# Second FFN of a hybrid block: GpSimd gathers the rows of four experts, not six, before its first scatter

## What is computed

```
xn   = rmsnorm(x) * norm_weight              # 4096 tokens x 128
probs = softmax(xn @ router_weight.T + router_bias)   # 16 experts
_, idx = top_k(logits.T, 256)                # each expert picks 256 tokens
xe = xn[idx]                                 # 16 x 256 x 128
h  = gelu(xe @ fc1.T + fc1_bias)             # 512 wide
y  = h @ fc2.T + fc2_bias
output = zeros.at[idx].add(y * gates)        # scatter-add over the experts
output = output / sum of the gates           # where a token was picked
```

## Time and profile before

| | before |
|---|---|
| median of 3 runs | 690.29 us |
| the profiled execution's own time | 692.55 us |
| its span | 690.8 us |
| mean granted TensorE clock | 0.766 |
| busy: VectorE, TensorE, GpSimd, ScalarE | 61%, 55%, 52%, 32% |
| the second FFN's experts, first gather to last scatter | 566.6 to 684.9 us |
| the first FFN's experts, first gather to last scatter | 224.7 to 329.5 us |

### The profile page before, as it was taken

How to read it: one execution, slowest core, us unless ns; L and a number is a source line. 1 busy time by engine, 2 the same in 40 slices (tenths; PEclk the granted TensorE clock), 3 DMA queues, 4 the chain that set the end, 5 groups by cost and what they waited for, 6 DMA issues and landing times.

```text
span 690.8 us, 7820 instructions
## 1 busy us (share of the span) xinstructions
PE 378.1 (55%) x2174; PEld 267.7 (39%) x2174; DVE 421.5 (61%) x1220; ACT 219.6 (32%) x531; POOL 360.0 (52%) x390
## 2 busy tenths in 40 slices
PE   4896756074321688675035677775743218767630
PEld 3554422071110576664012344442421106756630
DVE  6788999997887222222357899899687863122110
ACT  2577000036741122222024344442167212312200
POOL 6037960004101768888216888888540025888753
PEclk9999878578555789998556778788765558988975
DMA  5870000006213223333918888888481141333322
GB/s 147 322 303 1 0 1 0 0 15 199 63 30 46 57 33 46 44 40 35 251 15 128 129 135 132 130 136 124 51 244 31 30 54 44 40 46 46 40 20 19
DMA packets 67401, 55.73 MB, mean 81 GB/s; under 512 B 18016, under 2 KB 55520, under 8 KB 66080
## 3 DMA queue, kind: packets, MB, share of 16 engines
q1 hardware_dynamic: 47744, 44.63, 30.2%
q0 software_dynamic: 11392, 9.05, 9.8%
q10 hardware_dynamic: 8224, 1.57, 1.5%
HBM read 22.73 MB, written 15.73 MB: 56 GB/s over the span
## 4 chain that ended last, share of the span: by engine, by line
DVE 27%; POOL 18%; issue 16%; DMA 15%; PE 14%; SPq 3%; ACT 3%; another core or an unknown queue 2%; DVEq 1%; ACTq 0%; POOLq 0%
DVE arena L1240 11%; DMA arena<-arena 6%; POOL out L538 6%; POOL acc L538 6%; POOL arena L525 3%; DVE tk L1245 3%; DMA out<-arena,idx 3%; DVE arena L1245 2%; DMA acc<-arena,idx 2%; PE ps L951 2%; POOL tb L601 2%; DVE bst L1252 2%; SPq L403 2%; PE ps L1053 2%
## 5 line engine op out<-in xcount | busy, mean ns | idle before, releaser
L1240 DVE TENSOR_TENSOR arena<-ps,arena 128x256 f32<-128x256 f32 (+1 forms) x84 | 35.4, 430 | 154.6 <-DMA out<-arena,idx 71.5
L767 ACT ACTIVATE arena<-ps,b 128x256 f32<-128x256 f32 x128 | 50.1, 474 | 140.4 <-PE ps L1112 114.8
L525 POOL DMA_INDIRECT arena<-tab,idx x64 | 62.6, 979 | 33.9 <-issue 18.9
L1112 PE MATMUL ps<-arena,f1w 128*128 128x256 f32 x256 | 70.8, 426 | 15.1 <-DVE arena L1244 11.7
L601 POOL TENSOR_TENSOR tb<-arena 128x512 f32<-128x512 f32 x64 | 70.7, 1123 | 7.2 <-PE ps L1173 6.6
L1122 PE MATMUL ps<-f2w,arena 128*128 128x128 f32 x512 | 67.8, 287 | 7.0 <-issue 4.9
L1122 PEld LDWEIGHTS ps<-f2w,arena 128*128 128x128 f32 x512 | 66.6, 203 | 10.9 <-issue 8.7
L538 POOL DMA_INDIRECT out<-arena,idx x32 | 50.9, 1592 | 26.5 <-DMA out<-arena,idx 11.0
L1112 PEld LDWEIGHTS ps<-arena,f1w 128*128 128x128 f32 x256 | 52.1, 214 | 24.5 <-DVE arena L1244 13.3
L538 POOL DMA_INDIRECT acc<-arena,idx x32 | 50.6, 1580 | 13.6 <-issue 7.9
L1240 DVE TENSOR_TENSOR arena<-arena 128x256 f32<-128x256 f32 (+21 forms) x107 | 56.0, 557 | 2.2
(11 more groups left out here) (267 smaller groups left out, 914.1 us busy)
## 6 DMA issues: line engine op xcount, KB each, us to landing
arena<-arena SPq DMA_DIRECT2D x64, 256.0 KB, 7.2
f1w<-in_f1T SPq DMA_DIRECT2D x4, 1024.0 KB, 12.1
f2w<-in_f2T SPq DMA_DIRECT2D x4, 1024.0 KB, 14.1
tab<-tb SPq DMA_DIRECT2D x8, 512.0 KB, 3.3
acc<-tb SPq DMA_DIRECT2D x8, 256.0 KB, 18.9
arena<-in_f2b SPq DMA_DIRECT2D x2, 1024.0 KB, 5.9
acc<-xs SPq DMA_DIRECT2D x8, 256.0 KB, 6.4
xs<-acc SPq DMA_DIRECT2D x8, 256.0 KB, 5.7
```

The source lines that it names most:

```text
L525: pool.indirect_dma_start(out=XE[:, e % RX, h, :], out_offset=None, in_=tab[f], in_offset=bass.IndirectOffsetOnAxis(ap=idx[:, i:i + 1], ax ...
L767: last = nc.scalar.activation(hT[:, e % 2, t, :], ps[:, 2 * (e % 2) + t // 2, (t % 2) * CAP:(t % 2 + 1) * CAP], ACT.Gelu, bias=b1[:, e, t: ...
L1112: last = nc.tensor.matmul(ps[:, 2 * (e % 2) + t // 2, (t % 2) * CAP:(t % 2 + 1) * CAP], f1w[:, e, t * P:(t + 1) * P], xeT[:, e % 2, :], st ...
L1240: return nc.vector.tensor_tensor(o, a, b, op)
```

## The change

`AHEAD[1]` becomes RX // 2 = 4, from RX - 2 = 6. In the second FFN eight gathers, not twelve, are issued before the first scatter; from there on the gathers behind scatter e are those of expert e+4, not e+6, and the last ones stand behind scatter 11, not 9. The first FFN and the ring size stay as they are.

```diff
         RX = 8
 
-        AHEAD = (RX - 1, RX - 2)
+        AHEAD = (RX - 1, RX // 2)
         XE = carve(RX * 2 * TW).rearrange("p (r h w) -> p r h w", r=RX, h=2)
```

## The result

| | before | after |
|---|---|---|
| median | 690.57 us (4 runs) | 702.66 us (4 runs, 702.06 to 704.52) |
| the profiled execution's own time, span | 692.55, 690.8 | 702.93, 701.1 |
| first gather of the second FFN | 566.61 | 565.28 |
| S(0), first scatter of expert 0 | 586.25 | 581.71 |
| S(12) - S(0) | 76.52 | 92.30 |

The change makes the kernel slower: ratio 1.0174, 95% interval 1.0150 to 1.0198, which is 12.1 us by the medians. The forecast was 698.4 us, in a range of 693.5 to 703.5; the median lies in it, 4.3 us above the forecast.

What follows compares the result with a forecast made beforehand. GpSimd's queue, and what it waits for, was taken to bound the second FFN. A loop over two experts adds 12.3 us and an earlier start saves 4.2, so +8.1 on 690.29 gives 698.4 us, range 693.5 to 703.5.

Steps and rivals of the forecast that it cites:

- tail: Second FFN, the last scatters from S(12) to S(15), each waiting for the previous landing: stays 18.8 us.
- its own bound: Second FFN, upper limit for the loop over two experts with TensorE at low clock: 15.0 us, giving 699.6.
- rival 1: Start of the second FFN: S(0) stays at 586.25, so only the +12.3 us remains, 702.6 us; chance 0.22.
- The repeated part: Second FFN, S(0) to S(12): six loops of 14.8 us, 88.8 against 76.5, so +12.3 us.
- GpSimd's answer: Second FFN, from VectorE's finished y to GpSimd's scatter: taken as 0.7 us, 0.30 at least.
- TensorE's turn: Second FFN, from an even expert's transposes to the end of y: 5.4 us, bounds 3.95 and 5.64.
- The clock feeds itself: Second FFN, TensorE: a low-clock loop leaves 4.4 us idle before the next even expert, bringing low clock again.
- Rival 2: Second FFN, TensorE: clock stays high after the first loop, +5.0 less 4.2, +0.8 us, 691.1; chance 0.08.
- The start: Second FFN, first scatter: with eight early gathers S(0) comes at 582.0, 4.2 us earlier; bounds 0 and 4.6.
- I read it as something that the gathers hold up: Both FFNs, VectorE's late y(0): the wait ends 2.4 to 3.0 us behind the last early gather.
- Moved gathers and waits: Second FFN: two gathers moved between scatters 10 to 12 cost 0.7 us alone, inside the loop's time; moved waits nothing.
- Rival 3: Second FFN: quick GpSimd reply and high clock, loop 12.95 us, +1.2, start gains 4.6, 686.9 us; chance 0.08.

Runs made afterwards that it cites:

- ahead3: Changed kernel with three experts gathered ahead in the second FFN instead of four: 799.18 us (one execution).
- ahead5: Changed kernel with five experts gathered ahead in the second FFN instead of four: 684.16 us against 683.75 for the kernel before, ratio 1.0012.
- ahead4_turn_last: Changed kernel with TensorE's second-FFN transposes of expert e+1 put behind the second product of e-1: 686.31 us against 683.99 for the kernel before, ratio 1.0022.
- ahead4_fill4: Changed kernel plus constant matmuls on TensorE, 4 per expert and 12 ahead of expert 4, into unused PSUM: 686.61 us, ratio 1.0030 to the kernel before.
- ahead7: Changed kernel with seven experts gathered ahead in the second FFN, one more than before: 686.15 us against 683.75 for the kernel before, ratio 1.0030.
- before_again: The kernel before, unedited, profiled again beside the variants: 685.14 us, ratio 1.0018.

## Why the prediction was right, and where its sum was off

The mechanism was right and so was the sign. By the two profiled executions the steps are:

| step | forecast | measured |
|---|---|---|
| start, S(0) behind the first gather | -4.2 | -3.2 (19.64 to 16.43) |
| S(12) - S(0) | +12.3 | +15.8 (76.52 to 92.30) |
| tail | 0 | -1.0 (18.76 to 17.79) |
| ahead of the first gather | 0 | -1.3 (566.61 to 565.28) |
| sum | +8.1 | +10.3 (own times: +10.4) |

By the medians it is 12.1: the profiled execution of before lay 2.0 us above its median of 690.57 and that of after only 0.3. The last two lines aren't the change's: the tail waits for landings, of which one took 4.25 us in the first profile and the others 3.2 to 3.4, and the first gather comes when the router is done.

That the time fell within the range is in part luck. The loop came out above its own bound (15.4 us per two experts against 15.0), for which the prediction gave 699.6, and the range reached to 703.5 for rival 1 and for an answer of 1.44 us in every loop, neither of which came. Rival 1's number, 702.6, is the measured one by coincidence: it had the loop 3.5 us too short and the start 3.2 us too late, in the main.

1. *The repeated part.* "That closes a loop over two experts" held term by term, and ahead3, ahead5 and ahead4_turn_last show it. Two terms were mis-sized. Of GpSimd's answer I took 0.7; in the loop it is 0.28 (y(2) ends at 596.36, S(2) is 596.64). Of TensorE's turn I took 5.4, "a little less than the two measured"; it is 5.76 to 5.79 and 6.82 to 6.86 in turn, mean 6.3. Together: 7.8 + 6.3 + 0.95 + 0.28 = 15.3, six of them 92. The bound of 5.64 that I gave wasn't one: it was read from low stretches of 3.4 us, one begun just before the transposes (their 0.69 us at 606.88 in place of 0.44), two while TensorE worked. In the changed kernel they last over 6 us; behind idle times of 4.5 us and more the clock is low from the first transpose on, and in every second turn it stays so through part of the second product (2.97 against 1.95 us).
2. *The clock feeds itself.* Shown: low in all six even turns, high in the odd ones of the profile, and 1.00 once the gap was filled, which took 13.7 us out of S(12) - S(0). That a low turn makes the gap ahead of the next even one is read from the rows (0.54 us idle ahead of expert 5, 4.53 ahead of 6), and no run tried it apart. Rival 2, a clock that stays high after the first loop, fell: all six even turns were low. Its loops were +5.0 us; with no low turn at all they would be six of 13.35, +3.6, and ahead4_fill4 measures +1.5 (78.23 against 76.70), mostly since GpSimd's answer is 0.3 and not 0.7.
3. *The start.* The step "I read it as something that the gathers hold up" failed. The changed kernel's start did come 3.2 us earlier and looked like a proof, but ahead7 and before_again have 14 and 12 gathers running in the second FFN, and 16 in the first, and no hold. So gathers alone don't make it; whether they had a part in it where it occurred stays open, for in the first two profiles it ended 2.4 to 3.0 us behind the last gather three times. Without the hold the gain is 0.8 us. Where the hold did go, the start still gained 1.0 us less than forecast: TensorE's product for y(0) ended 14.61 us behind the first gather in place of 13.75, as the clock stayed low longer (its first product took 3.62 us, not 3.03), and GpSimd's answer was 0.85, not 0.7. The Trainium skill (Runtime: NRT & Kernel Launch, section Instruction fetch mechanics) calls the crossing of a code block "mostly hidden"; before_again agrees: one packet of code moves there too, 13 to 14 us behind the first gather, and VectorE starts 0.04 us behind TensorE. The first profile doesn't show what else held it. Rival 1, the start that doesn't move, was wrong as to the first profiles, and close for the later ones: it gave +12.3, measured there is +14.2.
4. *Moved gathers and waits.* "alone they would cost ... 0.7 us": ahead4_turn_last moves the same gathers without the loop, and its S(12) - S(0) is 77.18 against 76.70 in before_again and 76.52 in the first profile, 0.5 to 0.7 more. The moved waits for indices and row buffers cost nothing, as said.
5. Rival 3, faster, fell on the clock and on the start. GpSimd's quick answer, on which it also rested, was right, and the loop of 12.95 us that it named is the 13.02 of ahead4_fill4; but its gain of 4.6 us at the start was 3.2 and 0.8, and with the high clock the program is still 2.4 us slower than the kernel before.

## What to carry to other kernels

How far to fetch ahead isn't read from how long the rows take to land alone, but also from the program order of whoever uses them: count how many turns later the result comes that the fetching queue itself waits for. Here "four ahead" was two ahead for that wait, and a loop of 15 us over two turns beat a queue of 6.4 us per turn; five ahead was enough. A queue that never waited before can hide a low clock of another engine fully, and pay for it fully once a loop closes through that engine.

## What the runs showed that wasn't expected

- The hold of VectorE, ScalarE and TensorE at y(0) of the first FFN, 8.7 us, and of the second, 3.5 us, is there in the first profile and absent in a later one of the same program (0.04 us). A wait whose releaser the profile can't name should be seen in a second execution, on another chip if there is one, before a gain is built on it.
- GpSimd's time from VectorE's last write to the start of an indirect DMA is 0.28 us in the loop. At S(0) it is 0.85 us in all nine profiles with three to five experts ahead, and 1.44 us in all three with six. Why it depends on that wasn't tried; it is 0.59 of the 0.8 us that the start gains without the hold.
- Late rows made TensorE's matmuls slower, which made the next rows later: TensorE's busy time between S(0) and S(12) went from 54.66 to 60.33 us with the same work in it but for the edges.
